# High and low parts of theta and z laid side by side, element by element

## The reference

```python
q = einsum('bchw,dc->bdhw', x, theta_w) + theta_b      # 256 planes, 1024 pixels
xpool = maxpool2x2(x)                                  # 256 pooled pixels
k = einsum('bchw,dc->bdhw', xpool, phi_w) + phi_b
v = einsum('bchw,dc->bdhw', xpool, g_w) + g_b
p = softmax(einsum('bdn,bdm->bnm', q, k) * 256 ** -0.5)
vp = einsum('bdm,bnm->bdn', v, p)
out = einsum('bdhw,cd->bchw', vp, z_w) + z_b + x
```

## Time and profile before

| what | value |
|---|---|
| median of three executions | 2043.92 us |
| the three executions | 2041.92, 2043.92, 2044.03 us |
| profiled execution, first to last instruction (span) | 2040.4 us |
| what lies around the span, against the median | 3.5 us |
| TensorE matmuls busy | 2026.8 us, 99% of the span |
| TensorE weight loads busy | 2024.5 us, 99% |
| DVE, ACT, POOL busy | 76%, 64%, 67% |
| matmuls, and as many weight loads | 17,790 |
| of these with theta as weights, with z as weights | 6,144 and 5,376 |

### The profile page before, as it was taken

One profiled execution on the slowest core, in us unless ns is written; L12 is line 12 of the kernel. 1 busy time (PEld: TensorE's weight loads), 2 busy tenths in 40 slices (PEclk: granted clock), 3 DMA queues, 4 the chain that ended last, 5 costly groups with the idle time before them and its releaser, 6 DMA issues.

```text
span 2040.4 us, 48999 instructions
## 1 busy us (share of the span) xinstructions
PE 2026.8 (99%) x17790; PEld 2024.5 (99%) x17790; DVE 1558.1 (76%) x2625; ACT 1300.0 (64%) x2228; POOL 1366.5 (67%) x828
## 2 busy tenths in 40 slices
PE   9999999999999999999999999999999999999998
PEld 9999999999999999999999999999999999999998
DVE  8878777787777877777877778777787777787777
ACT  6666666666566665666666666666666566666663
POOL 4577666776666766667766677666677666776663
PEclk9999999999999999999999999999999999999999
DMA  7565656746556565566565664656656556656554
GB/s 243 191 212 184 213 169 214 236 170 210 175 207 232 180 210 185 186 226 210 181 212 171 215 237 169 209 177 207 232 180 210 184 187 226 209 182 214 170 193 166
DMA packets 213963, 407.27 MB, mean 200 GB/s; under 512 B 12720, under 2 KB 17840, under 8 KB 213936
## 3 DMA queue, kind: packets, MB, share of 16 engines
q1 hardware_dynamic: 213792, 406.90, 59.0%
q10 hardware_dynamic: 144, 0.01, 0.0%
HBM read 272.64 MB, written 134.22 MB: 199 GB/s over the span
## 4 chain that ended last, share of the span: by engine, by line
PE 97%; DVE 2%; POOL 0%; DMA 0%; issue 0%; ACT 0%; SPq 0%; DVEq 0%; POOLq 0%
PE bank L967 97%; DVE x_top L755 0%; DVE pt_raw L736 0%; DMA x<-x 0%; DVE x_bot L755 0%; DVE pooled L708 0%; POOL att_lo L631 0%; POOL x_split_lo L613 0%; POOL att_f L626 0%; DVE x L755 0%; PE bank L974 0%; SPq L265 0%; DVE q_lo L714 0%; ACT att_hi L425 0%; DVE xp_lo L851 0%
## 5 line engine op out<-in xcount | busy, mean ns | idle before, releaser
L613 POOL TENSOR_TENSOR x_split_lo<-x,x_split_hi 128x1024 fp32r<-128x1024 f32 x255 | 614.6, 2417 | 248.4 <-ACT x_split_hi L386 226.7
L967 PE MATMUL bank<-x_split_hi,theta_hi 128*128 128x256 f32 x2048 | 565.8, 276 | 3.1 <-POOL x_split_lo L613 2.0
L967 PE MATMUL bank<-x_split_lo,theta_hi 128*128 128x256 f32 x2048 | 565.7, 276 | 0.0
L967 PE MATMUL bank<-x_split_hi,theta_lo 128*128 128x256 f32 x2048 | 565.7, 276 | 0.0
L967 PE MATMUL bank<-att_hi,z_hi 128*128 128x256 f32 x1792 | 495.4, 276 | 3.6 <-DVE x_bot L755 2.5
L967 PE MATMUL bank<-att_hi,z_lo 128*128 128x256 f32 x1792 | 494.9, 276 | 0.0
L967 PE MATMUL bank<-att_lo,z_hi 128*128 128x256 f32 x1792 | 494.9, 276 | 0.0
L736 DVE STREAM_TRANSPOSE pt_raw<-probs 32x256 f32<-32x256 f32 x1024 | 445.9, 435 | 18.4 <-ACT probs L489 1.8
L631 POOL TENSOR_TENSOR att_lo<-att_f,att_hi 128x768 fp32r<-128x768 f32 x191 | 282.6, 1487 | 159.4 <-ACT att_hi L425 159.4
L967 PEld LDWEIGHTS bank<-x_split_hi,theta_hi 128*128 128x128 f32 x2048 | 384.6, 188 | 3.5 <-issue 3.5
L967 PEld LDWEIGHTS bank<-x_split_hi,theta_lo 128*128 128x128 f32 x2048 | 384.6, 188 | 0.0
(11 more groups left out here) (76 smaller groups left out, 4390.0 us busy)
## 6 DMA issues: line engine op xcount, KB each, us to landing
x<-x SPq DMA_DIRECT2D x258, 512.0 KB, 3.9
x_top<-x SPq DMA_DIRECT2D x128, 512.0 KB, 7.0
out<-x_top SPq DMA_DIRECT2D x128, 512.0 KB, 3.3
x_bot<-x SPq DMA_DIRECT2D x126, 512.0 KB, 5.2
out<-x_bot SPq DMA_DIRECT2D x126, 512.0 KB, 6.6
x_top<-theta_wt SPq DMA_DIRECT2D x4, 256.0 KB, 5.4
x_top<-g_wt SPq DMA_DIRECT2D x4, 256.0 KB, 5.4
x_bot<-z_wt SPq DMA_DIRECT2D x4, 256.0 KB, 6.2
```

What stands on the lines that cost most here:

```text
L613: nc.gpsimd.tensor_tensor(flat(lo), flat(x_chunk(s, c)), raw(flat(hi)), ALU.subtract).then_inc(x_ready, 1)
L967: last = nc.tensor.matmul(dst, stationary(a), moving(b), start=start and n == 0, stop=stop and n == len(PRODUCTS) - 1, skip_group_check=re ...
```

## The change

theta and z each become one tile with a last dimension of two, and the high part and the low part are views of it that take every second element. Everything that reads or writes theta or z uses these views without a further change in the code: ACT writes the high parts with a step of two elements (8 bytes), DVE reads the high parts and writes the low parts with that step, and each weight load of theta or z takes 128 elements over 1,024 bytes of a partition in place of 512. The moving operands stay as they are. The tiles take as much memory as before, and no other tile moves.

```diff
+        def paired(name, shape):
+
+            tile = sb(name, shape + [2], f32r)
+            return [tile[:, :, :, HI], tile[:, :, :, LO]]
+
...
-        theta = [sb(f"theta_{s}", [P, KT, D], f32r) for s in ("hi", "lo")]
-        zw = [sb(f"z_{s}", [P, 7, TB * P], f32r) for s in ("hi", "lo")]
+        theta = paired("theta", [P, KT, D])
+        zw = paired("z", [P, 7, TB * P])
```

## The result

The changed kernel takes 2123.37 us (median of 4, 2122.15 to 2132.21), the kernel before it 2043.87 us on the same chip: a ratio of 1.040, 95% interval 1.038 to 1.042. It is slower by 4%, where the forecast was no change.

What follows compares the result with a forecast made beforehand. TensorE's matmul pitch, read as set by the weight loads, was taken to bound the kernel. Span 2040.4 us + 0 (loads) + 0 (copies) + 0 (addresses) + 3.5 us between span and median gave 2043.9 us; range 2030 to 2150.

Steps and rivals of the forecast that it cites:

- The weight loads: 11,520 TensorE loads of theta and z, read with a step of two: forecast 0, bounded above by +772 to +1256 us.
- The nearer row: TensorE's moving operand reads 1,024 bytes of a partition within 113.3 ns; taken as showing that the stepped load costs 0.
- the +0 at its edge: Weight loads of theta and z: by the SBUF page's rule of two hits per 16-byte line, the step adds +0.
- +806 us: Weight loads of theta and z: the DVE page's rule carried over, +70 ns for each of 11,520, about 2850 us.
- What bounds the kernel: TensorE's matmul pitch of 113.3 ns, read as set by the weight load, with 0 to 23 ns to spare.
- rival "faster": TensorE pitch: -8 us if the higher pitch ends (0.07), -44 us if loads stop setting the pitch (0.03).
- rival "a little slower": Theta and z loads conflict with the moving operand's reads: +52 us, or twice that, +104 us; chance 0.23.
- rival "much slower": Theta and z loads fetch single elements and their work doubles: +772 to +1256 us, 2816 to 3300 us; chance 0.17.
- The copies: ACT and DVE instructions that make theta and z: between 0 and +1.3 us, taken as 0.
- The addresses: Loads sweeping memory faster could move matmuls between the two pitches: at most +52 us or -8 us, taken as 0.
- Theta and z at 180 to 222 ns: Sign that the forecast is wrong in the load, while q, xp, vt and phi keep their pitch.
- at 117.8 ns: Sign that the forecast is a little wrong: theta and z at this pitch, or phi at 113.3.

## Why the prediction was wrong

**The weight loads: "I take 0" failed.** This is the step. Measured: 6.7 ns for each of 11,520 loads, 76.8 us; a load of 128 elements with a step of 2 takes 120 ns by itself, more than the 113.3 that it was thought to fit into. The nearer row was the right one to look at: the moving side does fetch 1,024 bytes in these 113 ns, and a load with a step of 2 fetches as many, at nearly the same rate per 16 bytes. But "asks for no more than the moving side already gets" was taken as "fits into 113.3 ns", without a number for what such a load takes. The trace of before held none. For the same 64 pieces the moving side needs 113.3 ns or less, 1.77 ns for each, and the load 1.88; why the load is a little slower the runs don't say. Its 120 ns hardly depend on the moving side, since they stay under 128 columns (119.8).

"SBUF — State Buffer" of the Trainium skill (Specifications) asks for two hits on a line of 16 bytes for full bandwidth. A step of 8 bytes gives just two and costs 6%; a step of 3, which gives fewer on average, 53%; one hit, 108%. The trace agrees with where the cliff begins and not with the +0 at its edge. The rule of the "Vector Engine (DVE) Microarchitecture Reference" of the Trainium skill (5.2), from which +806 us were estimated, does not carry over to a load of this step: it grew by 6.7 ns, not by 70.

**What bounds the kernel: right within 2 ns.** The pitch was read as the load's, with 0 to 23 ns to spare. Its own work is 111 ns, about 2 ns less than the pitch, and the reading that nothing else covers a longer load held. What was wrong is the 109.5 ns left to the matmul itself, worked out from columns alone: the last 2 ns of 113.3 go with the moving side, and 512 columns take 230 to 233 ns, where that way of reckoning gives 216. So the 44 us of the rival "faster" were not there to be had.

**The rival "a little slower" (0.23) had the right size and the wrong mechanism.** Its +52 to +104 us hold the +80, but it priced a conflict between the two streams by the 4.5 ns of the two pitches. The price stays under 128 moving columns, and so it is the load's own; that the size fits is luck. The rival "much slower" is what a step of 4 would do: 235 ns, more than twice a packed load.

**The copies: right.** About 0.05 us more on each of ACT's, nothing on DVE's, hidden in the same wait.

**The addresses: 0 was nearly right.** One tile in blocks costs nothing. But z's step makes phi and the products behind it exchange their pitches, +6.6 us net. That the two pitches could be moved at all was kept as a bound; the -8 us of "faster" for phi came true for phi (-6.3 us) and was more than paid back behind it (+13).

**The sign shown in advance.** "Theta and z at 180 to 222 ns" or "at 117.8 ns" were the two signs named for a wrong forecast; 120.0 ns lies between them, next to the second. That phi went to 113.3 ns was named too.

## What to carry to other kernels

Where a weight load stands on the path that sets the end, price its access by the pieces of 16 bytes that it touches (here 1.8 to 1.9 ns each) against its columns (0.87 to 0.92 ns each at the full clock), and take the longer: for fp32 a step of 2 is just above, a step of 4 doubles the load. The same count holds for the moving operand, and a wider one hides the load's. Before a load is priced at nothing, find a row in which the same engine is limited by what the load will need, or measure one; "the other stream does as much" is no number.

## What was not expected of the hardware

The time for a piece of 16 bytes does not follow the granted clock: 64 of them took 120 ns at 1.00 and at 0.50, while 64 columns went from 59 to 107 ns. Hence a step of 2, which costs 128 columns 6% at 2.4 GHz, cost 64 columns nothing at 1.2 GHz.

"TensorE: Matmul & The Clock Gate" of the Trainium skill (LDWEIGHTS) gives a load of P columns P / 1.2 ns; an estimate from it is 106.7 for 128. The packed rows at the full clock agree to 5 or 6 ns (111, 85 and 59 ns for 128, 96 and 64 columns); the rows with a step don't.

The same matmul has two pitches, 113.3 and 117.8 ns, at the same granted clock. One filler per image put about 15,000 matmuls on the higher one (+3.1%), and 128 bytes of small tiles in another place put all of them there (+3.3%). That is nearly what the change itself cost, from edits that do no work; a comparison of two layouts in which the loads stand on the path should read the pitch of untouched products as well.
